# Projections of q, k and v as three fp32r products, on one Trainium2 core

## What is computed

```python
h = _layernorm(x, axis=-1) * (1 + ca) + sa
def proj(W, bias):
    y = x @ W.T + bias          # x here is h
    return y.reshape(b, s, h, d).transpose(0, 2, 1, 3).reshape(b * h, s, d)
q = _phi(proj(Wq, bq))          # _phi(x) = elu(x) + 1
k = _phi(proj(Wk, bk))
v = proj(Wv, bv)
...
scores = jnp.where(mask, einsum('bqd,bkd->bqk', qi, ki), 0)
num = einsum('bqk,bkd->bqd', scores, vi) + einsum('bqd,bde->bqe', qi, S)
```

## Time and profile before

| what | value |
|---|---|
| median of 3 runs | 513.25 us (510.47 to 516.6) |
| the profiled execution | 512.24 us, of which 510.4 us are its span (first to last instruction) |
| TensorE busy | 405.6 us, 79% of the span |
| VectorE busy | 320.1 us, 63% |
| ScalarE busy | 190.1 us, 37% |
| GpSimd busy | 227.0 us, 44% |
| mean granted clock of TensorE | 0.930 of 2.4 GHz |

### The profile page before, as it was taken

How to read it: one execution, slowest core, us unless ns; L and a number is a source line. 1 busy time by engine, 2 the same in 40 slices (tenths; PEclk the granted TensorE clock), 3 DMA queues, 4 the chain that set the end, 5 groups by cost and what they waited for, 6 DMA issues and landing times.

```text
span 510.4 us, 9185 instructions
## 1 busy us (share of the span) xinstructions
PE 405.6 (79%) x3218; PEld 288.4 (57%) x3218; DVE 320.1 (63%) x857; ACT 190.1 (37%) x314; POOL 227.0 (44%) x267
## 2 busy tenths in 40 slices
PE   3776889899899898898898887874129999999750
PEld 0333555655655665665665655654128888888640
DVE  5452855777777777788788779382714666666420
ACT  1445325525525425526526521202114444444100
POOL 3051142172182182181181171505164888888654
PEclk9997999999999999999999999787558999999895
DMA  8103104103403403403403302308265777775443
GB/s 266 37 0 99 35 6 120 49 7 120 135 6 117 136 7 110 142 5 104 146 4 103 110 6 92 110 1 283 90 172 168 192 189 194 164 166 110 48 50 42
DMA packets 41042, 50.30 MB, mean 99 GB/s; under 512 B 6313, under 2 KB 32938, under 8 KB 41010
## 3 DMA queue, kind: packets, MB, share of 16 engines
q1 hardware_dynamic: 33842, 37.17, 23.1%
q0 software_dynamic: 7168, 12.72, 12.8%
HBM read 32.40 MB, written 17.48 MB: 98 GB/s over the span
## 4 chain that ended last, share of the span: by engine, by line
PE 50%; DVE 13%; POOL 10%; issue 10%; ACT 9%; DMA 4%; SPq 1%; POOLq 1%; ACTq 0%; DVEq 0%
PE bank L795 11%; POOL out L559 6%; PE bank L822 6%; PE quad L856 4%; PE bank L906 4%; PE bank L883 4%; PE bank L931 3%; ACT xhat L658 3%; PE bank L842 3%; PE bank L871 2%; DVE in_slot L1340 2%; POOL xg L546 2%; PE bank L789 2%; DMA x_sb<-x 1%; PE quad L1024 1%
## 5 line engine op out<-in xcount | busy, mean ns | idle before, releaser
L1210 DVE TENSOR_TENSOR sT<-quad,causal 128x1024 f32<-128x1024 f32 x64 | 75.2, 1217 | 16.9 <-PE quad L856 16.8
L473 POOL TENSOR_TENSOR kcum<-qT,kcum 128x512 f32<-128x512 f32 x16 | 20.4, 1278 | 107.1 <-DVE kcum L1184 107.1
L559 POOL DMA_INDIRECT out<-x,list_back x32 | 53.0, 1657 | 10.9 <-issue 7.4
L1024 PE MATMUL bank<-w_hi,in_hi 128*128 128x256 f32 x128 | 37.9, 296 | 8.8 <-DVE in_lo L1441 5.7
L883 PE MATMUL bank<-sT,v_pad 128*32 128x128 f32 x1024 | 41.7, 283 | 0.0
L724 ACT ACTIVATE in_hi<-quad 128x512 fp32r<-128x512 f32 x32 | 19.1, 598 | 58.9 <-PE quad L1026 58.1
L546 POOL DMA_INDIRECT xg<-token_rows,list_in x32 | 35.0, 1093 | 13.1 <-issue 9.7
L906 PE MATMUL bank<-wog,oT 128*128 128x256 f32 x128 | 35.0, 397 | 7.2 <-DVE oT L1200 7.2
L856 PE MATMUL quad<-q_bd,kT 32*128 32x256 f32 x512 | 39.6, 416 | 0.4 <-DVE sT L1210 0.4
L1441 DVE SCALAR_TENSOR_TENSOR in_lo<-quad,in_hi 128x512 fp32r<-128x512 f32 x32 | 22.1, 692 | 24.0 <-ACT in_hi L724 22.2
L1026 PE MATMUL bank<-w_lo,in_hi 128*128 128x256 f32 x128 | 36.9, 288 | 0.0
(11 more groups left out here) (176 smaller groups left out, 947.5 us busy)
## 6 DMA issues: line engine op xcount, KB each, us to landing
token_rows<-h SPq DMA_DIRECT2D x8, 528.0 KB, 3.1
x_sb<-x SPq DMA_DIRECT2D x8, 512.0 KB, 4.2
rden<-rden_rows SPq DMA_DIRECT2D x64, 64.0 KB, 2.3
out<-x SPq DMA_DIRECT2D x8, 512.0 KB, 5.0
token_rows<-mod_all SPq DMA_DIRECT2D x8, 512.0 KB, 4.1
w_sb<-w1T SPq DMA_DIRECT2D x8, 512.0 KB
w_sb<-w2T SPq DMA_DIRECT2D x8, 512.0 KB
mod_all<-mod_rows SPq DMA_DIRECT2D x8, 384.0 KB, 5.3
```

Of the source, the lines that this page charges most:

```text
L559: gp.indirect_dma_start(out=out_rows, out_offset=bass.IndirectOffsetOnAxis(ap=list_back[q][:, t:t + 1], axis=0), in_=y_sb[q][:, t, :], in_ ...
L1024: mm(out, a_hi, b_hi, start=first, stop=False)
L1210: v.tensor_tensor(sT[t % 2][:, 8 * a:8 * (a + 1), :].rearrange("p (r s) i -> p r (s i)", s=2), quad[:, 2 * a:2 * a + 2, :].rearrange("p r ...
```

## The change

The weights of q, k and v are loaded into a borrowed buffer (`rden`) and split once: ScalarE writes the high part in fp32r (`wqkv_hi`), VectorE the rest (`wqkv_lo`). In each step ScalarE writes the modulated norm twice, rounded to fp32r (`h1_hi`) and in fp32 (`h1T`), and VectorE subtracts them into `h1_lo`. Each projection is then the sum of three fp32r products: high by high, high by low, low by high. The lists of TensorE and VectorE change at the head of the step. Besides, many calls of `wait(...)` are written as `wait_ge(...)` directly, which gives the same waits and isn't shown.

```diff
-        wq_sb, wk_sb, wv_sb, wo_sb = (sb(f"w{c}_sb", [P, KH, D]) for c in "qkvo")
+        wo_sb = sb("wo_sb", [P, KH, D])
+        wqkv_hi, wqkv_lo = (sb(f"wqkv_{part}", [P, 3, KH, D], F32R) for part in ("hi", "lo"))
...
+        h1_hi, h1_lo = (first(f"h1_{part}", [P, KH, SEQ], F32R) for part in ("hi", "lo"))
...
+        wqkv_sb = [rden[j // 2][:, j % 2, :].rearrange("p (k d) -> p k d", k=KH) for j in range(3)]
...
+            def split_weights():
+                wait(act, S["w_in"], 16 * 7)
+                for j in range(3):
+                    act.activation(wqkv_hi[:, j, :, :], wqkv_sb[j], ACT.Copy).then_inc(S["qkv_hi_on"], 1)
...
             def front_h(b):
                 for k in range(KH):
...
+                    act.wait_ge(S["h_mm"], KH * b.n + k + 1)
+                    act.activation(h1_hi[:, k, :], ring[k][:, :], ACT.Identity,
+                                   bias=mod_T[:, 0, k, bass.ds(b.n, 1)],
+                                   scale=mod_T[:, 1, k, bass.ds(b.n, 1)]).then_inc(S["h1_hi_on"], 1)
+                for k in range(KH):
                     act.activation(h1T[:, k, :], ring[k][:, :], ACT.Identity,
...
-            def project(to, w, m):
-                for k in range(KH):
-                    last = mm(to[:, :], w[:, k, m * P:(m + 1) * P], h1T[:, k, :],
-                              start=(k == 0), stop=(k == KH - 1))
-                return last
+            def project(to, b, j, m):
+
+                def part(w, h, first=False, last=False):
+                    for k in range(KH):
+                        ins = mm(to[:, :], w[:, j, k, m * P:(m + 1) * P], h[:, k, :],
+                                 start=(first and k == 0), stop=(last and k == KH - 1))
+                    return ins
+                part(wqkv_hi, h1_hi, first=True)
+                part(wqkv_lo, h1_hi)
+                pe.wait_ge(S["h1_lo_on"], KH * (b.n + 1))
+                return part(wqkv_hi, h1_lo, last=True)
...
                 if m == 1:
-                    wait(pe, S["h1T_on"], KH * (b.n + 1))
+                    if isinstance(b.n, int) and b.n == 0:
+                        wait(pe, S["qkv_lo_on"], 3)
+                    pe.wait_ge(S["h1_hi_on"], KH * (b.n + 1))
+                    pe.wait_ge(S["h1T_on"], KH * b.n + 1)
...
                 for t in range(2):
-                    for k in range(KH):
-                        last = mm(V_BANK[r][:, t * D:(t + 1) * D], h1T[:, k, tok(2 * r + t)],
-                                  wv_sb[:, k, :], start=(k == 0), stop=(k == KH - 1))
+                    for i, (h, w) in enumerate(((h1_hi, wqkv_hi), (h1_lo, wqkv_hi), (h1_hi, wqkv_lo))):
+                        for k in range(KH):
+                            last = mm(V_BANK[r][:, t * D:(t + 1) * D], h[:, k, tok(2 * r + t)],
+                                      w[:, 2, k, :], start=(i == 0 and k == 0), stop=(i == 2 and k == KH - 1))
...
+            def h_low(b):
+                for k in range(KH):
+                    dve.wait_ge(S["h1T_on"], KH * b.n + k + 1)
+                    v.tensor_tensor(h1_lo[:, k, :], h1T[:, k, :], full(h1_hi[:, k, :]), ALU.subtract)\
+                        .then_inc(S["h1_lo_on"], 1)
```

More of the change, by code:

```diff
@@ L516, in row_h @@
                     .then_inc(S["h2_on"], 1)
-                wait(gp, S["h2_on"], b.n + 1)
+                gp.wait_ge(S["h2_on"], b.n + 1)
                 gp.tensor_tensor(h2[:, :, 0:D], h2[:, :, 0:D],
@@ L608, in exp_min @@
                                scale=-1.0).then_inc(S[done], 1)
-                wait(act, S[done], count + 1)
+                act.wait_ge(S[done], count + 1)
                 act.activation(out[:, k, :], out[:, k, :], ACT.Exp, scale=-1.0).then_inc(S[done], 1)
@@ L613, in exp_q @@
                 done = KH * b.n + Q_ORDER.index(k)
-                wait(act, S["q_mm"], done + 1)
+                act.wait_ge(S["q_mm"], done + 1)
                 exp_min(0, q_exp, k, Q_BANK[k], "q_expd", 2 * done)
@@ L618, in exp_k @@
                 done = KH * b.n + k
-                wait(act, S["k_mm"], done + 1)
+                act.wait_ge(S["k_mm"], done + 1)
                 exp_min(1, k_exp, k, K_BANK[k], "k_expd", 2 * done)
             def spread_q(b):
-                wait(act, S["q_on"], KH * (b.n + 1))
+                act.wait_ge(S["q_on"], KH * (b.n + 1))
                 wait(act, S["sc_on"], TILES * 2 * (b.n - 1))
@@ L631, in front_v @@
                 for r in range(2):
-                    wait(act, S["v_mm"], 2 * b.n + r + 1)
+                    act.wait_ge(S["v_mm"], 2 * b.n + r + 1)
                     for t in range(2):
@@ L639, in front_kt @@
             def front_kt(b, r):
-                wait(act, S["kt_mm"], 2 * b.n + r + 1)
+                act.wait_ge(S["kt_mm"], 2 * b.n + r + 1)
                 n = 2 if r == 0 else TILES - 3
@@ L646, in front_den @@
             def front_den(b):
-                wait(act, S["den_mm"], b.n + 1)
+                act.wait_ge(S["den_mm"], b.n + 1)
                 wait(act, den_out, 16 * b.n)
@@ L652, in normalise_x1 @@
             def normalise_x1(b):
-                wait(act, S["rstd2_on"], 4 * (b.n + 1))
+                act.wait_ge(S["rstd2_on"], 4 * (b.n + 1))
                 wait(act, S["rh_mm"], KH * b.n)
@@ L911, in route_h @@
                 if k == 1:
-                    wait(pe, S["xhat_on"], TILES * (b.n + 1))
+                    pe.wait_ge(S["xhat_on"], TILES * (b.n + 1))
                     if front:
-                        wait(pe, S["k_on"], KH * front.n + 1)
+                        pe.wait_ge(S["k_on"], KH * front.n + 1)
                     else:
@@ L917, in route_h @@
                 elif front:
-                    wait(pe, S["q_on"], KH * (front.n + 1))
+                    pe.wait_ge(S["q_on"], KH * (front.n + 1))
                 else:
@@ L927, in route_logits @@
             def route_logits(b):
-                wait(pe, S["h2T_on"], KH * (b.n + 1))
+                pe.wait_ge(S["h2T_on"], KH * (b.n + 1))
                 for t in range(TILES):
@@ L935, in route_counts @@
             def route_counts(b, front):
-                wait(pe, S["oh_on"], b.n + 1)
+                pe.wait_ge(S["oh_on"], b.n + 1)
                 wait(pe, S["carry_on"], b.n)
                 if front:
-                    wait(pe, S["k_tok_on"], 2 * front.n + 1)
+                    pe.wait_ge(S["k_tok_on"], 2 * front.n + 1)
                 n = TILES * EXPERTS
@@ L952, in route_lists @@
             def route_lists(b):
-                wait(pe, S["slots_on"], b.n + 1)
+                pe.wait_ge(S["slots_on"], b.n + 1)
                 for c in range(2 * TILES):
@@ L1158, in setup, with split_weights @@
                 v.tensor_copy(bo_all[:, :], bank[2][:, 0:D]).then_inc(S["bo_on"], 1)
+            def split_weights():
+                for j in range(3):
+                    dve.wait_ge(S["qkv_hi_on"], j + 1)
+                    v.tensor_tensor(wqkv_lo[:, j, :, :], wqkv_sb[j], full(wqkv_hi[:, j, :, :]), ALU.subtract)\
+                        .then_inc(S["qkv_lo_on"], 1)
+            def h_low(b):
[3 more added lines that the diff above has]
+                        .then_inc(S["h1_lo_on"], 1)
             def early_stats(b):
-                wait(dve, x_in[b.p], 16 * (b.h + 1))
+                dve.wait_ge(x_in[b.p], 16 * (b.h + 1))
                 for t in range(TILES):
@@ L1169, in q_max @@
                 done = KH * b.n + Q_ORDER.index(k)
-                wait(dve, S["q_expd"], 2 * done + 2)
+                dve.wait_ge(S["q_expd"], 2 * done + 2)
                 v.scalar_tensor_tensor(out=qT[b.p][:, k, :], in0=Q_BANK[k][:, :], scalar=bias_p1[:, 0, k:k + 1],
@@ L1180, in k_sum @@
             def k_sum(b, k):
-                wait(dve, S["k_on"], KH * b.n + k + 1)
+                dve.wait_ge(S["k_on"], KH * b.n + k + 1)
                 wait(dve, S["den_mm"], b.n)
@@ L1187, in invert_den @@
             def invert_den(b):
-                wait(dve, den_in, 16 * (b.n + 1))
+                dve.wait_ge(den_in, 16 * (b.n + 1))
                 wait(dve, rden_out, 16 * b.n)
@@ L1251, in keep_logits @@
             def keep_logits(b):
-                wait(dve, S["lg_mm"], b.n + 1)
+                dve.wait_ge(S["lg_mm"], b.n + 1)
                 v.tensor_copy(logits[:, :, :],
@@ L1358, in step @@
                         setup()
+                        split_weights()
+                    h_low(front)
                 if attend:
```

150 lines of the change are left out of this document (76 added, 74 removed).

## The result

The changed kernel takes 528.05 us (median of five runs, 524.96 to 528.94) against 513.25 us before (510.47 to 516.6): ratio 1.0266, interval 1.021 to 1.0323. The profiled run of it took 524.96 us with a span of 523.2 us, 12.8 us more than the span before (510.4). It is the fastest of the five, at a mean granted clock of 0.915; the other four, of which there is no trace, took 527.66 to 528.94 us at 0.906 or 0.907. I forecast 522.5 us, in a range of 511.5 to 531.

The account below looks back on a forecast made before the run. TensorE was taken to set the pace, in turns with VectorE and ScalarE. 512.24 less 1.2 (first steps) plus 2.1 (six routing steps) gave 513.1; 9.4 for clock falls made 522.5 us, range 511.5 to 531.

Parts of the forecast that it names:

- The verdict: Whole kernel: slower by over 1%, given a chance of 0.64.
- The sign of being wrong that the prediction named last: Steps over 1 us longer at full clock, meaning something behind q, exponentials or second tile's mask has less slack.
- The pause: TensorE waits 2.8 us for h1_lo in the middle of q, in each step that routes.
- The walk of VectorE: Mask starts at 2.7 us in the step, means end at 6.25, subtractions at 7.5; TensorE gets h1_lo at 7.6.
- The clock: Clock falls behind five of seven pauses in the batch pipeline, 1.9 us each, 9.4 us in all.
- Rival (a): Clock stays in the batch pipeline; only 0.35 us a step remain: 513.1 us, bounds 510.5 to 515.8; chance 0.27.
- The step at full clock: End of v 0.35 us late and the next step as late; 2.1 us over six steps with a routed batch.
- The first steps: Two first steps, with no residual to wait for: v's saving wins 0.6 us each, 1.2 us together.
- (b): Subtraction on VectorE not late, or pause filled, so q, k and v's saving arrives: 496 us; chance 0.06.
- (c): Clock falls at each pause and stays down 6.8 us or more: 24 us, 537 us; chance 0.07 with (d).
- (d): TensorE's fp32r matmul takes as long as an fp32 record, 0.45 us: some 555 us; chance 0.07 with (c).

Follow-up runs that it names:

- the pause filled: Changed kernel with ten throw-away matmuls on TensorE before the third product of q's first half, all waits kept: 521.63 us.
- the order alone: Kernel before with only TensorE's list reordered as in the changed kernel, fp32 products and no subtraction: 514.14 us.
- h_lo first: Changed kernel with VectorE's two subtractions moved ahead of the mask of the attended batch's first tile: 508.27 us.
- the wide operations spread: GpSimd's row_h ahead of the second half of q times kcum, bias add onto x one step sooner: 526.72 us on the changed kernel, 503.88 on h_lo first.
- v high only: h_lo first with v made of the high by high product alone: 509.24 us; the same with the wide operations spread: 502.57 us.
- row_h early: h_lo first with GpSimd's row_h moved ahead of the second half of q times kcum: 506.41 us.

## Why the prediction was right, and where not

The verdict, the pause, its place and the fall of the clock held. The path from the pause to the next step did not, and the size, 9.3 us forecast and 14.8 measured, came together from terms that were off in both directions. That 528 lies within 511.5 to 531 is in part luck: by the prediction the changed kernel without a fall of the clock takes 510.5 to 515.8 us, and with the pause filled it took 521.63. The sign of being wrong that the prediction named last, steps longer at full clock by over 1 us, is what the profile shows.

**The pause.** Forecast 2.8 us in the middle of q in every step that routes; measured 2.40 (seven times 2.0 to 2.5). The walk of VectorE was right, with the subtractions ending at 7.43 in the step instead of 7.5, and TensorE going on at 7.48 instead of 7.6. The idle time released by the subtraction is 16.5 us, within the 15 to 20 forecast. That the order alone costs nothing and that h_lo first removes the pause shows its cause.

**The clock.** Forecast: five of seven pauses fall, 1.9 us each. Five of seven did in the profiled run; the other four runs had a lower mean clock, and how many fell there no trace shows. A fall cost 1.1 to 1.3 us in a routing step (2.6 to 2.7 more than before, for 1.4 to 1.5), since part of the slow stretch lies in the pause itself: 130.30 to 133.70 begins 0.6 us before the products go on. So by these steps the term is some 6 us for five, not 9.4, and filling the pause gave back 6.4. Rival (a) is out for the whole, though two steps behaved like it. The Trainium skill ("TensorE: Matmul & The Clock Gate", section "Why this matters for your kernels") advises against idle gaps between bursts of matmuls that are longer than any of these pauses. Here gaps of 2.4 were enough in five cases and in all seven of the changed kernel with the wide operations spread, so it can't be read as leave to have shorter ones.

What the prediction put forward for (a), that pauses up to 2.28 us left the clock alone, is not so in the trace it was read from. A pause of 1.78 us stands there ahead of 10.2 us at half clock, which the prediction leaves out:

```profile
324.45 1.13 PE L906 MATMUL bank<-wog,oT 128*128 128x256 f32 x4 [1.78 <-DVE oT L1200]
```
```profile
325.90:336.10 10.20, 9.62 (x69) 7.07 (x68) 4.87 (x26) 0.21 (x1) 0.58 (x1) 0.50 0.05 16
```

**The step at full clock.** This is the term that was mis-sized: "at the end of v the step is 0.35 us late ... and the next step starts as late", 6 x 0.35 = 2.1 us. Measured: 1.4 to 1.5 in each of the five steps that can be read, some 7 us where the prediction has 1.75. Two things were wrong. First, a half of q or k takes 1.50 us (257.12 to 258.62), not 1.36: two of its pairs stand 0.46 to 0.47 before what follows, and the one next to matmuls of another kind 0.56 to 0.57. A half of v takes 1.50 to 1.52, not 1.44. At the end of v TensorE is 0.88 us late, not 0.35. Second, the end of v doesn't set the next step. VectorE's queue from k's maximum does, and k was 1.50 late (1.10 in my walk). I had checked that TensorE is busy without a break behind v up to the numerators, but not what it waits for behind them: before the change already 0.35, 0.81 and 0.89 us for VectorE, the last time ahead of the lists (272.49); after it 0.35, 1.44 and 0.89. VectorE was itself busy from the maximum to the lists. What v saved became time in which VectorE stood behind GpSimd; the two kernels with v high only, without and with the spreading, show it.

**The first steps and the rest.** Forecast: 1.2 us won in the two first steps. Measured from start to start, they lost 0.74 and 1.80 us, and the first transposes start 0.23 late. In the second a pause of 2.01 us opens at 51.56, and half clock follows it; I had counted the fall, not the delay. From the last of these starts (286.55) to the end the changed kernel is 0.9 us shorter than the one before. The sixth routing step lies there, and a drain behind it, in which nothing enters the pipeline any more. The step takes 43.24 us up to its lists, 39.29 before: 3.95 more, at a granted clock of 0.91 for 1.00. The drain, from these lists to those of the next batch, takes 28.55 us at 0.96, 32.69 at 0.84 before: 4.14 less. So more of the half clock lies in the drain before and in the step after, and the shorter drain hides what the sixth step cost. With the five steps (2.70 + 2.67 + 1.44 + 2.62 + 1.51) the sum is 12.8, the difference of the spans.

**The other rivals.** (b) is what h_lo first does, and it shows that the 496 us I gave it were too low: the pause goes, and TensorE then waits 1.04 us for q's maximum and VectorE for GpSimd, so 508.3 are reached, 503.9 with the spreading. The steps of h_lo first are as long as before; its gain, 4.8 us in the medians and 3.3 in the profiles (spans 510.4 and 507.1), lies outside of them: 0.6 us in the five steps, 3.9 in the drain (28.75 us at a granted clock of 0.97, for 32.69 at 0.84), and 2.0 lost in the sixth step (41.29 for 39.29, at 0.90 for 1.00). Over all fourteen profiles the drain takes 28.3 to 29.6 us at 0.89 to 1.00 and 31.4 to 34.4 at 0.79 to 0.84, so a few us of any total here hang on where the clock falls, and the steps compare the kernels better. (c) and (d) didn't come; the products' spacing was 0.47 a pair for the 0.45 forecast, but for the pairs next to other matmuls.

## What to carry to other kernels

Before giving a saving on one engine to the step, follow what the next step's first instruction waits for, back to a point where an engine really starts fresh: here that was VectorE's maximum of k, not the end of v. If edits on one engine leave the time from some point on the same to 0.03 us, look for operations there that end together with another engine's. An operand split into parts needs its low part as early as its first product needs it, so the subtraction belongs ahead of the longer work on its engine; and an idle gap in TensorE's stream can cost its clock as well as its time, so judge it by both.

## What the runs showed of the hardware

Some VectorE operations end only when GpSimd's wide one does. The conversion of 128x8 took 0.15 us with GpSimd idle or at narrow work, and 0.52, 1.14, 1.72 and 2.26 us with a wide operation under way, each time to within 0.05 us of its end; the slot product took 0.22, and 0.44 to 1.76 to within 0.09 us of its end. The mask, whose data come from PSUM, kept 1.22 us for each of its two operations beside the wide pass of row_h (249.29 and 249.24 in the kernel with row_h early), and the statistics their 0.43 beside it (274.39 after the change). It goes the other way too: GpSimd's dummy operation of one column took 1.15 us at 252.83, to within 0.05 us of the end of VectorE's subtraction, and 0.38 at 275.81. The Trainium skill ("SBUF — State Buffer", section "Who interferes with whom") says so: the two engines share a pair of ports as an exclusive lock, and VectorE operations with two SBUF inputs, or casts in a two-port mode, take it. Every case above agrees; in which mode the conversion ran no trace shows.

Pauses of one length, in one place of the step, 2.40 us, were followed by half clock in some steps and not in others of the same run, and in every step of another kernel (all seven with the wide operations spread). Shorter ones did both too: one of 1.81 us ahead of the output projection left the clock at 1.00 in the kernel before (306.66) and was followed by half clock in the one with the order alone (306.99). One of 1.56 us was followed by half clock too (332.53 in the kernel with h_lo first and row_h early). From these traces a forecast can count such falls only as a chance.
